# Attention inside two chained mixture-of-experts blocks: routing in front of the second head's scores, the product in front of the second turn, a batch's first output product later, and each pair's blocks read back at once

## The chip, the cores and the metric

The kernel runs on one core of one Trainium2 chip. The metric is the device time of one execution in microseconds, from three runs; each run is one execution of the whole program. TensorE is called PE in the profile, VectorE DVE, ScalarE ACT, GpSimd POOL, SyncE SP.

## The reference

Input x is 8 batches of 256 tokens of width 256. Two layers follow each other; each is x + FFN(COND(x)).

```python
x = x + L0_ffn(L0_cond(x, cond_64, ...), ...)      # MoE with 8 experts (A), MoE with 8 experts (B)
x = x + L1_ffn(L1_cond(x, fside, mask, ...), ...)  # attention (C), MoE with 16 experts (D)

def L1_cond(x, attn_bias, mask, g_in, null_attn_bias, null_kv, Wq, Wkv, Wo, g_out):
    xn = layernorm(x, g_in)                        # 16 query heads of width 64, one key/value head
    q = heads(xn @ Wq) * scale
    k, v = null row in front of (xn @ Wkv)         # 257 keys
    sim = q @ k.T + bias; sim = causal mask, key mask -> lowest
    out = softmax(sim) @ v
    return layernorm(heads together (out) @ Wo, g_out)
```

L1_ffn picks two of 16 experts for each token from the attention's output (its routing), so the routing of D for a batch can begin as soon as that batch's attention is done.

## The kernel before, in words

Everything is written by hand for each engine: an engine's program is one straight list, and semaphores order the engines among each other. Stages A and B come first; stage C (attention) takes the span from about 380 to 690 us; D follows.

Stage C treats one batch after the other (`batches`), and in a batch the heads in eight pairs, j = 0 to 7; p = 8b + j counts the 64 pairs. Each engine has a function for a batch (`pe_batch`, `act_batch`, `dve_batch`, `pool_batch`) whose loop over j is a software pipeline. In place p stand these steps:

- PE: scores of pair p+1 into psH or psHT (L1491), the sum (weights times values) of pair p-3 into psL (L1504, `pe_sum`, LAG = 3), queries of pair p+3 into psY (L1477), the output product of pair p-4 accumulated in psM (L1515, `pe_out`). The first output product of a batch has to wait until VectorE has read the previous batch's psM out (L1881, semaphore out_raw).
- DVE: transposes of the exponentials of pair p, head 1 (`dve_blocks`, L1863), scores plus bias with their minimum for pair p+1, head 1 (`dve_scores`, L1838), blocks of head 0 (L1863), reciprocals of the sums (L1845) and their transposes (L1852), the scaling of pair p-3's sum into c_oT (`dve_o`, L1872), scores of pair p+1, head 0, and last a piece of D's routing (`dve_dispatch`, L1917 to L1989). In some places the layer norm's statistics come between (`dve_row_*` L1799 to L1814, `dve_out_*` L1885 to L1900).
- ACT: exponentials of pair p+1, head 1 and head 0 (L1706), between them the copy of the queries (L1700), in some places normalization of rows (L1672), a copy for the routing (L1727), the mask (L1693) and the normalization of the outputs (L1680).
- POOL: mask minus bias of pair p+2, both heads (L2181), gating of the next batch's rows (L2195, L2199), rstd by a power (L2204, L2214), the weighting with g_out (L2225) and the indirect DMAs that dispatch tokens (L2247).
- SP: a transpose over 128 partitions is made of VectorE's transposes of 32x32 blocks and a trip through DRAM. `sp_store_blocks(p)` (L2341) writes the 512 KB of pair p from c_x1 to DRAM once the last transposes of the pair are done (128 rows, 4 KB each). `sp_load_blocks(p)` (L2350) reads them back in another order into c_x2 (512 pieces of 1 KB); it waits for the store to have landed and for the scaling of pair p-2, which frees the buffer. c_x1 and c_x2 have two buffers each; DVE's first transpose of pair p waits until store p-2 has landed.

SP's program for the stage is one list:

```python
for p in range(pairs):
    sp_store_blocks(sp, p)
    if p >= 1:
        sp_load_blocks(sp, p - 1)
```

Other DMAs run at the same time: expert weights of D on ACT's queue in batch 0 (one piece a pair), 4 MB of them on SP's queue in front of the first store, two loads of 256 KB a batch (L1723, ACT's queue), and four indirect DMAs a batch (POOL's queue).

Of the kernel before, what the change touches and what calls it, by code (L numbers as in the profile page):

```python
# [14 lines left out]
P = 128  # L15
# [212 lines left out]
def build(nc, io):  # L228
    ctx = ExitStack()
    with ctx:  # L230
# [6 lines left out]
        def carve(region, sizes):  # L237
# [81 lines left out]
            work, [512, 1024, 512, 4 * KEYS, 2 * KEYS, 4 * KEYS, DIM, 512, KEYS, 24, 1024, 2 * QT * DH, 4])  # L319
# [10 lines left out]
        c_oT = c_oT.rearrange("p (r n) -> p r n", r=2)  # L330
# [1177 lines left out]
        def pe_out(pe, p, j, b):  # L1508


            pe.wait_ge(C.o_ready, p + 1)
            if j == 0:
                wait(pe, C.out_raw, 2 * b)
            for i in range(QT):
                last = pe.matmul(psM[:, i * DIM:(i + 1) * DIM], c_oT[:, j % 2, i * P:(i + 1) * P], c_wo[:, j, :],  # L1515
                                 start=(j == 0 and i == 0), stop=(j == NPAIR - 1), skip_group_check=True)
            last.then_inc(C.wo_mm, 1)
# [90 lines left out]
        def pe_batch(pe, b, odd, first, last):  # L1608
            for j in range(NPAIR):
# [4 lines left out]
                if s >= 0:  # L1614
                    pe_sum(pe, s, s % NPAIR, s // NPAIR)
                if j == 1 and b >= 3:
                    pe_z_counts(pe, b - 3, psX)
# [15 lines left out]
                if s >= 1:  # L1633
                    pe_out(pe, s - 1, (s - 1) % NPAIR, (s - 1) // NPAIR)
# [107 lines left out]
        def act_batch(act, b, odd, first, last):  # L1742
            for j in range(NPAIR):
# [4 lines left out]
                if j == 3 and not last:  # L1748
                    act_normal_rows(act, b + 1)
                if j == 4 and not last:  # L1750
                    act_rowsT(act, b + 1, 1 - odd)
                if not (last and j + 3 >= NPAIR):
                    act_queries(act, p + 3, j + 3)
                if more:
                    act_exp(act, p + 1, j + 1, ORDER[1])
                act_load_d(act, p)
# [7 lines left out]
                if j == 2 and b >= 2:  # L1764
                    act_zT(act, b - 2)
# [100 lines left out]
        def dve_o(dve, p, j):  # L1866
# [4 lines left out]
            wait(dve, C.wo_mm, p - 1)  # L1871
            nc.vector.tensor_tensor(c_oT[:, j % 2, :].rearrange("p (i a q) -> p i a q", i=QT, a=4),  # L1872
# [186 lines left out]
        def dve_dispatch(dve, b, j, last):  # L2059
# [6 lines left out]
            if j == 2 and b >= 3:  # L2066
                dve_dest(dve, b - 3)
            if j == 3 and b >= 3:
                dve_counted(dve, b - 3)
            if j == 4 and b >= 2:  # L2070
                dve_best(dve, b - 2, 0)
            if j == 5 and b >= 2:
                dve_onehot(dve, b - 2, 0)
            if j == (5 if last else 6) and b >= 2:
                dve_best(dve, b - 2, 1)
            if j == (5 if last else 7) and b >= 2:
# [8 lines left out]
        def dve_batch(dve, b, odd, first, last):  # L2085
            for j in range(NPAIR):
# [7 lines left out]
                if j == 3 and not last:  # L2094
                    dve.wait_ge(C.row_step, 4 * b + 6)
                    dve_row_moments(dve, b + 1)
                    dve_row_variances(dve, b + 1)
                if more:
                    dve_scores_wait(dve, p + 1)
                    dve_scores(dve, p + 1, j + 1, ORDER[0])  # L2100
                dve_blocks(dve, p, j, ORDER[1])
                dve_sums(dve, p, j)
                dve_recs(dve, p)
                if s >= 0:
                    dve_o(dve, s, s % NPAIR)
                if j == 4 and not first:
                    dve_out_raw(dve, b - 1)

                if j == 2 and not last:
                    dve.wait_ge(B.combined, 2 * b + 4)  # L2110
                    dve_row_stats(dve, b + 1)
                if j == 5 and not first:
                    dve.wait_ge(C.out_step, 4 * b - 2)
                    dve_out_moments(dve, b - 1)
                    dve_out_variances(dve, b - 1)
                if more:
                    dve_scores(dve, p + 1, j + 1, ORDER[1])
                if j == 4 and not first:
                    dve.wait_ge(C.out_raw, 2 * b)
                    dve_out_stats(dve, b - 1)  # L2120
                if j == 3 and not last:
                    dve_row_shift(dve, b + 1)
                if j == 5 and not first:
                    dve_out_shift(dve, b - 1)
                dve_dispatch(dve, b, j, last)
# [124 lines left out]
        def pool_batch(pool, b, odd, first, last):  # L2250
            for j in range(NPAIR):
                p = 8 * b + j
                over = (j + 2) // NPAIR
                for n, o in enumerate(ORDER):
# [9 lines left out]
                    if h <= 2 * QT and not last:  # L2264
                        pool_pairs(pool, b + 1, h)
                    if j == 4 and n == 0:
# [12 lines left out]
                if j == 3 and not last:  # L2279
                    pool_row_rstd(pool, b + 1)  # L2280
# [72 lines left out]
        def sp_attention(sp):  # L2353
# [7 lines left out]
            for p in range(pairs):  # L2361
                sp_store_blocks(sp, p)
                if p >= 1:
                    sp_load_blocks(sp, p - 1)
            sp_load_blocks(sp, pairs - 1)
# [318 lines left out]
```

## Time and profile before

| what | us |
|---|---|
| three runs | 855.49, 839.8, 849.12 |
| their median | 849.12 |
| the profiled execution | 854.32 |
| its span, first to last instruction | 852.6 |
| mean granted clock of TensorE (share of full speed) | 0.92 |

The rows further down come from that one profiled execution. A row of a group or a timeline names line, engine, operation, and "written tile <- read tiles"; "x8" is a count, and brackets hold the idle time of the engine before it with what ended it. "PEclk" is the granted TensorE clock as a share of full speed. The queue q1 in the DMA view is SP's, q10 is ACT's, q0 is POOL's.

### The profile page before, as it was taken

What the parts mean: (1) busy time and instruction counts of PE and PEld (TensorE: products, weight loads), DVE (VectorE), ACT (ScalarE), POOL (GpSimd) and SP (SyncE); (2) the same over time, 40 slices, a digit from 0 to 9 for tenths busy, and PEclk for the clock granted to TensorE, in tenths of its full rate; (3) what the DMA queues carried; (4) which work ended last, traced back from release to release, by engine and by line L of the source; (5) the groups of instructions that cost most, each with busy time, mean ns of one, the idle gap of its engine ahead of it and who ended that gap; (6) DMA issues with size and microseconds to landing.
All of it is one profiled execution on the core that took longest, in us unless ns stands there. A gap on an engine that the chain in (4) does not pass through costs nothing. (4 is left out here: it accounts for less than half of the span.)

```text
span 852.6 us, 15701 instructions
## 1 busy us (share of the span) xinstructions
PE 737.8 (87%) x4481; PEld 568.2 (67%) x4482; DVE 476.1 (56%) x1751; ACT 361.0 (42%) x1068; POOL 422.6 (50%) x506
## 2 busy tenths in 40 slices
PE   8859995966999989985899989899989688988788
PEld 5349964655999989863566656566666445877665
DVE  2704464464232222246778899988989742444346
ACT  3526621233222222245546655565656315665302
POOL 1166315414453863245638486867857431344530
PEclk9889997966999999998999999999999778999979
DMA  9634533325979666188977777778868743444346
GB/s 315 257 99 143 136 111 112 100 87 166 351 255 356 215 180 205 56 296 309 336 260 246 240 237 249 253 249 265 264 205 273 237 148 96 119 122 139 107 142 197
DMA packets 101035, 173.41 MB, mean 203 GB/s; under 512 B 10976, under 2 KB 77792, under 8 KB 99936
## 3 DMA queue, kind: packets, MB, share of 16 engines
q1 hardware_dynamic: 79392, 117.03, 41.7%
q0 software_dynamic: 10944, 30.03, 11.5%
q10 hardware_dynamic: 10624, 25.46, 8.7%
q8 instruction: 34, 0.56, 0.3%
q14 instruction: 41, 0.34, 0.1%
HBM read 111.86 MB, written 60.62 MB: 202 GB/s over the span
## 5 line engine op out<-in xcount | busy, mean ns | idle before, releaser
L2181 POOL TENSOR_TENSOR work<-work,region_ac 128x386 f32<-128x386 f32 x128 | 119.4, 941 | 69.3 <-ACT work L1693 32.9
L1706 ACT ACTIVATE work<-work 128x129 f32<-128x129 f32 (+1 forms) x256 | 114.2, 448 | 89.2 <-DVE work L1838 87.3
L1863 DVE STREAM_TRANSPOSE region_bd<-work 128x384 f32<-128x384 f32 x128 | 73.3, 572 | 12.2 <-ACT work L1706 6.3
L1515 PE MATMUL psM<-region_ac,work 128*128 128x256 f32 x256 | 71.1, 403 | 9.7 <-DVE acc L1881 9.7
L1504 PE MATMUL psL<-region_bd,work 128*64 128x256 f32 (+1 forms) x512 | 61.6, 365 | 19.0 <-DMA region_bd<-c_blocks 17.0
L1367 POOL DMA_INDIRECT d_pairs<-work,home x47 | 45.9, 976 | 64.0 <-DVE home_f L1119 44.9
L1477 PE MATMUL psY<-work,region_ac 128*128 128x256 f32 x256 | 71.3, 401 | 2.2 <-ACT work L1700 2.2
L1504 PEld LDWEIGHTS psL<-region_bd,work 128*64 128x64 f32 x512 | 34.1, 147 | 55.1 <-DMA region_bd<-c_blocks 27.2
L1356 POOL DMA_INDIRECT b_pairs<-work,home x39 | 38.1, 977 | 56.9 <-DVE work L1063 54.6
L860 PE MATMUL psH<-work,region_bd 128*128 128x128 f32 x472 | 62.8, 290 | 3.9 <-ACT work L968 2.2
L1348 POOL DMA_INDIRECT work<-in_x,inv x39 | 37.1, 953 | 55.5 <-DVE inv L1276 35.0
L1037 ACT ACTIVATE work<-work 128x512 f32<-128x512 f32 x39 | 24.6, 630 | 93.6 <-DVE work L1056 70.4
L860 PEld LDWEIGHTS psH<-work,region_bd 128*128 128x128 f32 x472 | 59.8, 205 | 5.7 <-ACT work L968 3.4
L1515 PEld LDWEIGHTS psM<-region_ac,work 128*128 128x128 f32 x256 | 50.0, 200 | 19.7 <-DVE work L1872 10.9
L1429 POOL DMA_INDIRECT work<-a_slots,slot_u x32 | 31.3, 978 | 48.1 <-DMA a_slots<-work 26.7
L1348 POOL DMA_INDIRECT work<-y_scratch,inv x39 | 37.8, 968 | 35.0 <-DVE inv L1276 21.4
L1477 PEld LDWEIGHTS psY<-work,region_ac 128*128 128x128 f32 x256 | 44.0, 192 | 12.2 <-issue 4.8
L1838 DVE CUSTOM_DVE_ANT_0 work<-psHT,work 128x129 f32<-128x129 f32 (+1 forms) x128 | 40.2, 350 | 17.9 <-PE psHT L1491 16.6
L1706 ACT ACTIVATION_READ_ACCUMULATOR work<-work 128x1 f32 x256 | 47.9, 187 | 0.0
L1838 DVE CUSTOM_DVE_ANT_0 work<-psH,work 128x129 f32<-128x129 f32 (+1 forms) x128 | 40.1, 350 | 4.9 <-PE psH L1491 4.7
L913 PE MATMUL psHT<-work,region_bd 128*128 128x128 f32 x304 | 37.6, 276 | 4.6 <-ACT work L1026 3.4
L913 PE MATMUL psH<-work,region_bd 128*128 128x128 f32 x320 | 41.3, 285 | 0.0
(367 smaller groups left out, 1608.3 us busy)
## 6 DMA issues: line engine op xcount, KB each, us to landing
c_blocks<-region_bd SPq DMA_DIRECT2D x64, 512.0 KB
region_bd<-c_blocks SPq DMA_DIRECT2D x64, 512.0 KB
region_bd<-in_b_w ACTq DMA_DIRECT2D x37, 512.0 KB
work<-d_rows SPq DMA_DIRECT2D x47, 132.0 KB
a_slots<-work SPq DMA_DIRECT2D x19, 256.0 KB
region_bd<-in_b_w SPq DMA_DIRECT2D x1, 4096.0 KB, 15.4
region_bd<-in_d_w SPq DMA_DIRECT2D x1, 4096.0 KB, 19.7
work<-d_pairs SPq DMA_DIRECT2D x16, 256.0 KB
```

The source lines that it names most:

```text
L860: last = pe.matmul(pair_h[p % DEEP][:, t % PAIR, j, :], f.w_in(j, k, t), xT[:, p % DEEP, t % PAIR, k, :], start=(k == 0), stop=(k == KD - 1))
L913: last = pe.matmul(ffn_h[u % RING][:, j * P:(j + 1) * P], f.w_in(j, k, u % RING), b_xT[:, u % 2, k, :], start=(k == 0), stop=(k == KD - 1))
L1348: pool.indirect_dma_start(out=slot_rows(f, t), out_offset=None, in_=st.src, in_offset=bass.IndirectOffsetOnAxis(ap=inv[:, t:t + 1], axis=0 ...
L1356: pool.indirect_dma_start(out=st.pair_dram, out_offset=bass.IndirectOffsetOnAxis(ap=home[:, t:t + 1], axis=0), in_=ys[:, t % RING, :], in_ ...
L1367: pool.indirect_dma_start(out=st.pair_dram, out_offset=bass.IndirectOffsetOnAxis(ap=home[:, t:t + 1], axis=0), in_=d_ys[:, t % ROWS, :], i ...
L1477: last = pe.matmul(psY[:, 0:SEQ], c_wq[:, c, j * P:(j + 1) * P], c_xnT[:, odd, c, :], start=(c == 0), stop=(c == KD - 1))
L1504: last = pe.matmul(psL[DH * o:DH * o + DH, queries].rearrange("p (i a q) -> p i a q", a=4, q=32), c_v[:, b % 2, n, :], weights[:, o, block ...
L1515: last = pe.matmul(psM[:, i * DIM:(i + 1) * DIM], c_oT[:, j % 2, i * P:(i + 1) * P], c_wo[:, j, :], start=(j == 0 and i == 0), stop=(j == ...
L1706: nc.scalar.activation(c_p[:, j % 2, o, a:z], c_sc[:, o, a:z], ACT.Exp, scale=-1.0, bias=c_min[:, o, i:i + 1], accum_out=c_sum[:, j % 2, o ...
L1838: last = nc.vector.tensor_tensor_reduce(c_sc[:, o, a:z], psS[j % 2][:, o, a:z], c_bm[:, 2 * (j % 2) + o, a:z], 1.0, -LOWEST, ALU.add, ALU. ...
L1863: nc.vector.transpose(out=c_x1[:, p % 2, :, (QT + 1) * o:(QT + 1) * (o + 1), :].rearrange("p b i q -> p i b q"), in_=c_p[:, j % 2, o, 1:1 ...
L2181: pool.tensor_tensor(c_bm[:, 2 * (j % 2) + o, :], c_mp, c_bias[:, 2 * j + o, :], ALU.subtract).then_inc(C.bm_ready, 1)
```

## The change

- SP reads a pair's blocks back directly behind their store: store(p), load(p), store(p+1), and so on.
- DVE scales the sum of pair p-3 in front of the blocks of head 0 instead of behind the reciprocals. c_oT has three buffers instead of two, and `dve_o` waits for the output product of three pairs ago.
- DVE's routing step stands in front of the scores of head 0. Its pieces are spread anew: destinations in place 1 instead of 2, first choice in 5 and 6 instead of 4 and 5, second choice in 7 instead of 6 and 7.
- The statistics of the next batch's rows are taken in place 2 behind the scores, moments and variances with them (before: place 3); POOL's rstd stands between its two steps in place 3.
- ACT normalizes the next batch's rows behind the exponentials of head 0 in place 3, and copies for the routing in front of them in place 2.
- PE leaves out the output product in place 4 (a batch's first) and makes it in place 5, in front of the next one.

The core of the diff:

```diff
-            work, [512, 1024, 512, 4 * KEYS, 2 * KEYS, 4 * KEYS, DIM, 512, KEYS, 24, 1024, 2 * QT * DH, 4])
+            work, [512, 1024, 512, 4 * KEYS, 2 * KEYS, 4 * KEYS, DIM, 3 * SEQ, KEYS, 24, 1024, 2 * QT * DH, 4])
...
-                last = pe.matmul(psM[:, i * DIM:(i + 1) * DIM], c_oT[:, j % 2, i * P:(i + 1) * P], c_wo[:, j, :],
+                last = pe.matmul(psM[:, i * DIM:(i + 1) * DIM], c_oT[:, p % 3, i * P:(i + 1) * P], c_wo[:, j, :],
...
+                if j == 5:
+                    pe_out(pe, 8 * b, 0, b)
...
-                if s >= 1:
+                if s >= 1 and j != 4:
                     pe_out(pe, s - 1, (s - 1) % NPAIR, (s - 1) // NPAIR)
...
-                if j == 3 and not last:
-                    act_normal_rows(act, b + 1)
...
+                if j == 2 and b >= 2:
+                    act_zT(act, b - 2)
                 if more:
                     act_exp(act, p + 1, j + 1, ORDER[1])
+                if j == 3 and not last:
+                    act_normal_rows(act, b + 1)
...
-                if j == 2 and b >= 2:
-                    act_zT(act, b - 2)
...
-            wait(dve, C.wo_mm, p - 1)
+            wait(dve, C.wo_mm, p - 2)
...
-            if j == 2 and b >= 3:
                 dve_dest(dve, b - 3)
...
-            if j == 4 and b >= 2:
+            if j == 5 and b >= 2:
                 dve_best(dve, b - 2, 0)
-            if j == 5 and b >= 2:
+            if j == (5 if last else 6) and b >= 2:
                 dve_onehot(dve, b - 2, 0)
-            if j == (5 if last else 6) and b >= 2:
+            if j == (5 if last else 7) and b >= 2:
                 dve_best(dve, b - 2, 1)
-            if j == (5 if last else 7) and b >= 2:
                 dve_onehot(dve, b - 2, 1)
...
-                if j == 3 and not last:
-                    dve.wait_ge(C.row_step, 4 * b + 6)
-                    dve_row_moments(dve, b + 1)
-                    dve_row_variances(dve, b + 1)
                 if more:
                     dve_scores_wait(dve, p + 1)
                     dve_scores(dve, p + 1, j + 1, ORDER[0])
+                if s >= 0:
+                    dve_o(dve, s, s % NPAIR)
                 dve_blocks(dve, p, j, ORDER[1])
                 dve_sums(dve, p, j)
                 dve_recs(dve, p)
-                if s >= 0:
-                    dve_o(dve, s, s % NPAIR)
                 if j == 4 and not first:
                     dve_out_raw(dve, b - 1)
-
-                if j == 2 and not last:
-                    dve.wait_ge(B.combined, 2 * b + 4)
-                    dve_row_stats(dve, b + 1)
                 if j == 5 and not first:
                     dve.wait_ge(C.out_step, 4 * b - 2)
                     dve_out_moments(dve, b - 1)
                     dve_out_variances(dve, b - 1)
+                dve_dispatch(dve, b, j, last)
+                if j == 3 and not last:
+                    dve_row_shift(dve, b + 1)
                 if more:
                     dve_scores(dve, p + 1, j + 1, ORDER[1])
+                if j == 2 and not last:
+                    dve.wait_ge(B.combined, 2 * b + 4)
+                    dve_row_stats(dve, b + 1)
+                    dve.wait_ge(C.row_step, 4 * b + 6)
+                    dve_row_moments(dve, b + 1)
+                    dve_row_variances(dve, b + 1)
...
-                if j == 3 and not last:
-                    dve_row_shift(dve, b + 1)
...
-                dve_dispatch(dve, b, j, last)
...
+                    if j == 3 and n == 0 and not last:
+                        pool_row_rstd(pool, b + 1)
...
-                if j == 3 and not last:
-                    pool_row_rstd(pool, b + 1)
...
             for p in range(pairs):
                 sp_store_blocks(sp, p)
-                if p >= 1:
-                    sp_load_blocks(sp, p - 1)
-            sp_load_blocks(sp, pairs - 1)
+                sp_load_blocks(sp, p)
```

## Rows read from the trace of the kernel before

**Rows 1.** The page, section 1: busy time of each engine over the span.
```profile
PE 737.8 (87%) x4481; PEld 568.2 (67%) x4482; DVE 476.1 (56%) x1751; ACT 361.0 (42%) x1068; POOL 422.6 (50%) x506
```

**Rows 2.** Table of stretches, batches 0 and 4: length, busy us (instructions) by engine, clock, DMA.
```profile
381.35:419.21 37.86, 27.07 (x169) 18.34 (x170) 25.52 (x117) 20.24 (x79) 22.81 (x30) 0.91 0.94 331
...
531.67:569.94 38.27, 34.30 (x225) 23.69 (x224) 34.18 (x150) 21.96 (x83) 28.39 (x37) 0.96 0.76 248
```

**Rows 3.** The stores' line by itself: duration ns, first and last start us.
```profile
L2341 SPq DMA_DIRECT2D c_blocks<-region_bd x64: 319/319/333, 381.3 to 674.8; - x64
```

**Rows 4.** Timeline of TensorE, 595 to 603: start us, duration us, then the group.
```profile
595.42 0.93 PE L1491 MATMUL psHT<-region_bd,work 64*128 64x129 f32 x8
...
599.00 0.93 PE L1491 MATMUL psH<-region_bd,work 64*128 64x129 f32 x8
```

**Rows 5.** Waits (us in total, times, longest) and one routing group, 380 to 690.
```profile
DVE work L1838 <- PE psHT L1491: 16.6, 15, 2.5
DVE region_bd L1863 <- ACT work L1706: 5.2, 6, 1.1
PE psL L1504 <- DMA region_bd<-c_blocks: 17.0, 12, 7.9
PE psM L1515 <- DVE acc L1881: 9.7, 7, 2.0
...
L1933 DVE TENSOR_TENSOR region_bd<-region_bd 128x32 f32<-128x32 f32 x12 | 6.4, 532 | 0.4
```

**Rows 6.** Timeline, 574 to 580, and the table of stretches behind it (clock: third figure from the right).
```profile
574.21 0.39 SPq L2350 DMA_DIRECT2D region_bd<-c_blocks  x1
...
579.96 0.87 PE L1504 MATMUL psL<-region_bd,work 128*64 128x256 f32 x8 [1.35 <-DMA region_bd<-c_blocks]
...
582.00:584.00 2.00, 2.00 (x7) 1.62 (x6) 1.97 (x12) 0.99 (x4) 2.00 (x4) 0.58 0.03 13
```

**Rows 7.** Timeline of SyncE's queue, 598 to 602, and its waits in the stage.
```profile
598.15 0.32 SPq L2341 DMA_DIRECT2D c_blocks<-region_bd  x1
598.57 0.40 SPq L2350 DMA_DIRECT2D region_bd<-c_blocks  x1
601.74 0.32 SPq L2341 DMA_DIRECT2D c_blocks<-region_bd  x1
...
SPq L2350 <- DMA c_blocks<-region_bd: 8.0, 4, 5.9
```

**Rows 8.** DMA view of 598.9 to 600.5, then of 600.5 to 602.4: packets by size.
```profile
DMA packets 135, 0.52 MB, mean 328 GB/s; under 512 B 2, under 2 KB 10, under 8 KB 134
...
DMA packets 539, 0.54 MB, mean 285 GB/s; under 512 B 30, under 2 KB 534, under 8 KB 538
```

**Rows 9.** Timeline, 381 to 394: the first two stores, the first load, the first sum.
```profile
381.35 3.10 SPq L2341 DMA_DIRECT2D c_blocks<-region_bd  x2
390.34 0.37 SPq L2350 DMA_DIRECT2D region_bd<-c_blocks  x1
...
394.11 1.12 PE L1504 MATMUL psL<-region_bd,work 128*64 128x256 f32 x4 [7.89 <-DMA region_bd<-c_blocks]
```

**Rows 10.** Timeline, 419 to 428: a load, the store behind it, and what each releases.
```profile
419.63 0.39 SPq L2350 DMA_DIRECT2D region_bd<-c_blocks  x1
...
422.80 0.32 SPq L2341 DMA_DIRECT2D c_blocks<-region_bd  x1
...
426.32 0.87 PE L1504 MATMUL psL<-region_bd,work 128*64 128x256 f32 x8 [1.75 <-DMA region_bd<-c_blocks]
...
428.07 0.37 SPq L2350 DMA_DIRECT2D region_bd<-c_blocks  x1
```

**Rows 11.** DMA queues, 380 to 690: packets, MB, share of 16 engines.
```profile
q10 hardware_dynamic: 4992, 6.05, 5.6%
q0 software_dynamic: 1152, 3.25, 2.9%
```

**Rows 12.** Timeline, 674 to 688: the last store and the last sum.
```profile
674.82 0.32 SPq L2341 DMA_DIRECT2D c_blocks<-region_bd  x1
...
687.60 1.12 PE L1504 MATMUL psL<-region_bd,work 128*64 128x256 f32 x8
```

More of the change, by code:

```diff
@@ L329, in build @@
         c_p = c_p.rearrange("p (r o n) -> p r o n", r=2, o=2)
-        c_oT = c_oT.rearrange("p (r n) -> p r n", r=2)
+        c_oT = c_oT.rearrange("p (r n) -> p r n", r=3)
         c_min = c_small[:, 0:4].rearrange("p (o i) -> p o i", o=2)
@@ L1870, in dve_o @@
             wait_dma(dve, C.blocks_loaded, 0, p)
-            wait(dve, C.wo_mm, p - 1)
-            nc.vector.tensor_tensor(c_oT[:, j % 2, :].rearrange("p (i a q) -> p i a q", i=QT, a=4),
+            wait(dve, C.wo_mm, p - 2)
+            nc.vector.tensor_tensor(c_oT[:, p % 3, :].rearrange("p (i a q) -> p i a q", i=QT, a=4),
                                     psL[:, 0:SEQ].rearrange("p (i a q) -> p i a q", i=QT, a=4),
```

## The prediction

> **What bounds the kernel now.** I read the busy shares first. TensorE is busy for 87% of the span and no other engine for more than 56% [rows 1], but that mixes stages. The change touches only the attention stage, so the next view is the table of stretches there: in the fifth batch (531.67 to 569.94) TensorE is busy for 34.30 of 38.27 us and VectorE for 34.18 [rows 2]. Two engines are nearly full and neither is quite full, so they take turns waiting. SyncE's issue rows give the pace: 64 stores from 381.3 to 674.8, that is 293.5 us in 63 steps, 4.66 us a pair [rows 3]. The timeline of TensorE shows what it could do: where nothing holds it, one pair's scores start at 595.42 and the next at 599.00, 3.58 us a pair [rows 4]. So about 1.1 us of each pair is lost somewhere.
>
> The waits say where. VectorE waits 16.6 us for the scores in psHT and 5.2 for exponentials; TensorE waits 17.0 us for the loaded blocks and 9.7 for VectorE to read psM out [rows 5]. One such wait can be followed: the load issued at 574.21 releases the product at 579.96 after 1.35 us of idleness, and shortly after, between 582 and 584, the granted clock is 0.58 instead of 1.00 (the lower level, 1.2 GHz, for most of it) [rows 6]. TensorE's pause thus costs twice. The transfers are late since SyncE issues the load of pair p only behind the store of pair p+1: store 598.15, load (of the pair before) 598.57, next store 601.74 [rows 7].
>
> **The change, part by part.**
>
> *Blocks read at once.* SyncE now runs store(p), load(p), store(p+1). Nothing is added in instructions or bytes: 64 stores and 64 loads of 512 KB stay. What is added is a wait: load(p) waits for store(p) to land and for the product of pair p-2 to have been scaled, and SyncE is in order, so store(p+1) is queued behind that wait. VectorE's transposes of pair p+3 wait for store(p+1), TensorE's sum for its load. In the old order this wait was nearly always over when it was reached, because a whole pair lay between.
>
> How long is one turn of this loop? It has three pieces.
> (a) A load that has the queue to itself. SyncE issues one at 390.34, and TensorE, idle for 7.89 us, is released by it at 394.11 [rows 9]: 3.77 us.
> (b) The store behind it. It is ready long before (VectorE's work is 34.2 us for 8 pairs [rows 2]), so it is issued at once, 0.42 us after the load (the distance of 598.15 and 598.57 is that of two issues in a row [rows 7]). Do its packets pass the load's? The windows of the DMA view say no, for the opposite order: the load is issued at 598.57, yet from 598.9 to 600.5 the packets are all but ten of the store's size (4 KB), and from 600.5 to 602.4, 534 of 539 are small ones, the load's [rows 8]. The queue is worked off in order. What a store costs behind a load is seen at 419 to 428: the load of 419.63 releases TensorE at 426.32, the store of 422.80 releases SyncE at 428.07 [rows 10], 1.75 us later.
> (c) SyncE's own issue times lie inside (a).
> A turn is so 3.77 + 1.75 = 5.5 us. By the other bound, if the store's packets didn't wait at all, a turn would be 0.42 us and a store alone: its packets end 2.35 us after its issue [rows 7, 8], so 2.8 us and a landing time the views do not show. I take 5.5: the rows in (b) are the same two transfers on the same queue.
> The order of packets is shown here for a load behind a store only. The Trainium skill, page "DMA: Bandwidth & Descriptors", section "Queues, rings and completion order", states it for every pair: on each engine the descriptors are consumed in ring order. By that rule a store waits for a load just as well; without it the turn could be as short as the lower bound above.
>
> 5.5 is above the 4.66 of today, and each pair needs one turn, so the loop sets the pace whatever the engines do. Sum: from the first store of batch 1 (419.21) to the last (674.82) there are 55 steps in 255.6 us; 55 x 5.5 = 302.5, +47. In batch 0 the first store, issued at 381.35, has landed at 390.34 (the 4 MB of expert weights go first), and now the second store, today issued by 384.45, waits for that [rows 9]. From 390.75 there are 7 turns to the first store of batch 1: 429.3 instead of 419.2, +10. Other queues take engine time too: 5.6% and 2.9% of the stage's 310 us [rows 11], 0.41 us a pair. Today it fits into gaps; in a closed loop up to two thirds of it count (the share of a turn in which the blocks' packets run), 0 to 17 us. I take 8. At the end, today 12.8 us lie between the last store and the last sum (674.82, 687.60) [rows 12]; then it is about 5.1 (store behind a load) + 3.8 (load alone), -4. Together +61 us.
>
> *Product in front of the second turn* (VectorE's scaling of the sum, L1872, moves in front of the blocks of head 0, with a third buffer for its result). The same 61 instructions. It lets load(p) go earlier by the length of a block's transposes and sums, and fills the time in which the exponentials of head 0 run, the cause of the 5.2 us [rows 5]. The price is a wait for the sum in front of the blocks, at most one sum of 0.87 us [rows 6]. Alone: from -5 (those waits gone) to +26 (half of the pairs wait a whole sum). In the loop of 5.5 us VectorE has the slack, so I count 0.
>
> *Routing in front of the second head's scores.* The same instructions in another place, destinations one pair earlier, second choices later. The scores of head 0 start later by the routing, and its exponentials with them. A single product of the first choice averages 532 ns [rows 5] over 12, so one pair's share is 0.5 to 1.5 us. 0 as long as VectorE waits for blocks anyway; if that cover were gone, up to 1 us in half of the pairs, +30, against what the removed waits give.
>
> *A batch's first outputs held back* (the first output product goes to place 5, two in one pair). It removes the 9.7 us in which TensorE waits for psM [rows 5] and adds nothing; TensorE has 1.9 us of slack in a 5.5 us pair. 0 here. The statistics of the next batch's rows behind the scores, their rstd earlier on GpSimd, the normalization and the turn's copy moved around ScalarE's exponentials: likewise 0 here; alone they would remove short waits of VectorE.
>
> The profiled execution took 854.32 us, the three runs have a median of 849.12. The sum is made against the profile: 854.3 + 61 = 915. Against the median: 849.1 + 61 = 910; since the natural 3.77 may have held some of the weights' traffic, I lower this slightly, to **906 us**.
>
> **Rivals.**
>
> *Faster: the removed waits count, the loop does not bind.* The place is SyncE's load issue. If a store behind a load landed within 4.2 us of its issue, a turn would be under 4.66. Then TensorE's 17.0 + 9.7 us, VectorE's 16.6 + 5.2 [rows 5] and the half-clock stretches would be open for gain. VectorE has 34.2 us of work in 38.3 [rows 2]; half of the difference over seven batches and what the first loses less gives -14 to -30: 827 us. For it: loads are the latest thing in the slowest places [rows 6]. Against it: the order of packets [rows 8] and the 1.75 us behind a load [rows 10]. The point from which it decides is a turn of 4.66 us.
>
> *No difference: the loop binds a little.* A turn of 4.4 to 4.9 us, if half of the store's transfer ran beside the load's (1.6 of 3.5 us of packets hidden). The pace stays at today's, the gains in the slow places pay for batch 0: 850 us.
>
> *Worse than forecast: the clock.* TensorE's pauses grow to 1.4 us or more in every pair, the length after which the clock fell at 582 [rows 6]. At the lower clock its pair needs about 7.2 us (twice 3.58), over 5.5. If a third of the pairs ran so, +35: 940. Against: batch 0 has a clock share of 0.91 although TensorE is idle for 10.8 us of it [rows 2].
>
> **How the numbers follow.** The loop as forecast 0.66 (its own range 885 to 930), with the clock on top 0.11, no difference 0.09, faster 0.14. The range leaves out the faster case and most of the clock's: 845 to 930. Two per cent is about what a measurement of this kernel can tell from no change: slower 0.77, same 0.09, faster 0.14.
>
> **What would show it.** Right: SyncE's load waits for its own store in nearly every pair (today 8.0 us in total, 4 times [rows 7]), store to store is 5.3 to 5.8 us in the steady batches, each store is issued 0.4 us after a load, VectorE's blocks wait for stores, and TensorE's wait for psM is gone. Wrong: stores less than 4.7 us apart; or a store that lands within 4 us though a load is just ahead of it; or a pace of 5.5 with waits that end at the sum or the scores instead of at the store.

## The result, and the profile after

The kernel with the change takes 923.43 us (median of 4 runs, 919.83 to 926.55), the kernel before 846.79 us beside it on the same chip (4 runs, 839.80 to 855.49). The ratio is 1.093, with a 95% interval of 1.084 to 1.102: 9.3% slower, 76.6 us by the medians. The profiled execution took 923.82 us, its span is 922.1 us, so profile against profile the loss is 922.1 - 852.6 = 69.5 us. Some executions of one kernel take longer as a whole than the rest (here 855.49 us of the kernel before), and the ratios and their intervals, in the whole document, are made without those, so a ratio can differ from the quotient of the two medians beside it.

The page's first section for the kernel after, which answers to [rows 1]:

```profile
PE 754.1 (82%) x4481; PEld 578.7 (63%) x4482; DVE 472.1 (51%) x1751; ACT 361.0 (39%) x1068; POOL 422.5 (46%) x506
```

No instruction was added. VectorE does the same work in a longer span. TensorE's busy time rose by 16 us with the same 4481 instructions: it ran more of them at the lower clock (mean granted clock 0.911, before 0.920). The stores' line by itself, against [rows 3]:

```profile
L2339 SPq DMA_DIRECT2D c_blocks<-region_bd x64: 319/457/815, 376.8 to 751.0; - x64
```

From the first store to the last it is now 374.2 us instead of 293.5, that is 5.94 us a pair instead of 4.66. These 80.7 us are more than the whole loss; what offsets the rest is listed further down, under "The sum". The waits of the stage say what each engine waits for (us in total, times, longest), against [rows 5] and the last of [rows 7]:

```profile
DVE region_bd L1865 <- DMA c_blocks<-region_bd: 115.9, 57, 6.3
PE psL L1504 <- DMA region_bd<-c_blocks: 84.4, 49, 9.0
DVE work L1840 <- PE psHT L1491: 0.3, 1, 0.3
...
SPq L2348 <- DMA c_blocks<-region_bd: 260.0, 60, 9.1
```

Before, VectorE's transposes (L1863, now L1865) did not wait for stores except once; now they do in 57 of 64 pairs. SyncE's load waits for its own store in 60 pairs, 260.0 us in all, where it was 8.0 us in 4. TensorE's wait for psM is gone, and VectorE's for the scores nearly so: both engines now arrive early at nearly everything except a transfer (VectorE's scaling still waits 8.8 us in 3 pairs for the sum). One turn and the start of the next, from the timeline at the start of the fifth batch (start us, duration us, what it is, in brackets the idle time before it and its releaser):

```profile
568.68 0.37 SPq L2348 DMA_DIRECT2D region_bd<-c_blocks  x1
568.76 0.58 DVE L1865 STREAM_TRANSPOSE region_bd<-work 128x384 f32<-128x384 f32 x1 [1.46 <-DMA c_blocks<-region_bd]
569.15 0.46 SPq L2339 DMA_DIRECT2D c_blocks<-region_bd  x1
...
573.16 1.20 PE L1504 MATMUL psL<-region_bd,work 128*64 128x256 f32 x8 [2.01 <-DMA region_bd<-c_blocks]
574.38 0.37 SPq L2348 DMA_DIRECT2D region_bd<-c_blocks  x1
574.46 0.58 DVE L1865 STREAM_TRANSPOSE region_bd<-work 128x384 f32<-128x384 f32 x1 [1.81 <-DMA c_blocks<-region_bd]
574.84 0.46 SPq L2339 DMA_DIRECT2D c_blocks<-region_bd  x1
```

Read it as a circle. The load goes out at 568.68 and the store of the next pair 0.47 us behind it. That store lands before 574.38; its landing releases both the next load (574.38) and VectorE's next transposes (574.46), since these write the buffer that the store reads. The load's landing releases the sum at 573.16. A turn is 574.38 - 568.68 = 5.70 us, and no step of the circle is computing. The DMA view of 569.7 to 571.9 and then of 571.9 to 574.2 shows the order of packets, in answer to [rows 8]:

```profile
DMA packets 329, 0.34 MB, mean 154 GB/s; under 512 B 1, under 2 KB 328, under 8 KB 329
...
DMA packets 343, 0.71 MB, mean 309 GB/s; under 512 B 31, under 2 KB 216, under 8 KB 343
```

The store was issued at 569.15, yet until 571.9 all but one of 329 packets are small ones, the load's. The store's large ones come as the load's run out: by the packet records the first starts at 571.77, the rest from 571.92 on, and the load's last ends at 572.76. So a store does wait for a load ahead of it, as a load does for a store in [rows 8]; that a ring's descriptors are consumed in order is also what the Trainium skill, page "DMA: Bandwidth & Descriptors", section "Queues, rings and completion order", states, and here the trace agrees.

### The profile page after: what moved, and what is told of

Read it like the earlier page. It is cut to its first block and busy times, and to the rows that moved or that the text cites. A ratio compares the mean times of both kernels' runs of the same rounds, so it can differ in the third digit from the quotient of the medians.

```text
span 922.1 us, 15701 instructions
## 1 busy us (share of the span) xinstructions
PE 754.1 (82%) x4481; PEld 578.7 (63%) x4482; DVE 472.1 (51%) x1751; ACT 361.0 (39%) x1068; POOL 422.5 (46%) x506
## 5 line engine op out<-in xcount | busy, mean ns | idle before, releaser
L1865 DVE STREAM_TRANSPOSE region_bd<-work 128x384 f32<-128x384 f32 x128 | 73.3, 573 | 117.1 <-DMA c_blocks<-region_bd 115.9
L1477 PE MATMUL psY<-work,region_ac 128*128 128x256 f32 x256 | 83.1, 454 | 2.1 <-ACT work L1702 2.1
L1515 PE MATMUL psM<-region_ac,work 128*128 128x256 f32 x256 | 79.9, 444 | 0.0
L1515 PEld LDWEIGHTS psM<-region_ac,work 128*128 128x128 f32 x256 | 56.7, 227 | 11.7 <-issue 2.4
L860 PEld LDWEIGHTS psH<-work,region_bd 128*128 128x128 f32 x472 | 59.6, 205 | 3.9 <-ACT work L968 2.3
L1477 PEld LDWEIGHTS psY<-work,region_ac 128*128 128x128 f32 x256 | 50.6, 219 | 14.3 <-issue 5.2
L913 PEld LDWEIGHTS psH<-work,region_bd 128*128 128x128 f32 x320 | 40.0, 203 | 1.9 <-issue 1.9
```

The lines of the kernel that those rows point to most:

```text
L860: last = pe.matmul(pair_h[p % DEEP][:, t % PAIR, j, :], f.w_in(j, k, t), xT[:, p % DEEP, t % PAIR, k, :], start=(k == 0), stop=(k == KD - 1))
L913: last = pe.matmul(ffn_h[u % RING][:, j * P:(j + 1) * P], f.w_in(j, k, u % RING), b_xT[:, u % 2, k, :], start=(k == 0), stop=(k == KD - 1))
L1477: last = pe.matmul(psY[:, 0:SEQ], c_wq[:, c, j * P:(j + 1) * P], c_xnT[:, odd, c, :], start=(c == 0), stop=(c == KD - 1))
L1515: last = pe.matmul(psM[:, i * DIM:(i + 1) * DIM], c_oT[:, p % 3, i * P:(i + 1) * P], c_wo[:, j, :], start=(j == 0 and i == 0), stop=(j == ...
L1865: nc.vector.transpose(out=c_x1[:, p % 2, :, (QT + 1) * o:(QT + 1) * (o + 1), :].rearrange("p b i q -> p i b q"), in_=c_p[:, j % 2, o, 1:1 ...
```

## The experiments

Each kernel was compared with the kernel before on one chip, but not all of them on the same one, and the kernel before is not equally long everywhere (842.80, 846.79 and 851.16 us, and 791.17 us beside experiments 5 to 8). So times are compared with the kernel before beside them, and stage lengths by the distance between stores.

**1. The order of reads alone.** The kernel before with this edit and nothing else:

```diff
             for p in range(pairs):
                 sp_store_blocks(sp, p)
-                if p >= 1:
-                    sp_load_blocks(sp, p - 1)
-            sp_load_blocks(sp, pairs - 1)
+                sp_load_blocks(sp, p)
```

> The kernel before with SyncE's new order alone (store p, load p); nothing else of the change. Theory (closed loop: the load waits for its own store, the next store is queued behind the load): stores 5.7 to 6.0 us apart, VectorE waiting for stores by about 100 us in the stage, time 915 to 930 us, the whole loss of the change. Rival (the loss comes from the moved engine steps, or from both together): below 890 us.

Measured: 927.90 us, before 851.16; ratio 1.101 (1.082 to 1.120). The stores' line by itself:

```profile
L2341 SPq DMA_DIRECT2D c_blocks<-region_bd x64: 319/457/1938, 377.0 to 751.9; - x64
```

and the waits of the stage:

```profile
DVE region_bd L1863 <- DMA c_blocks<-region_bd: 115.6, 57, 6.3
...
SPq L2350 <- DMA c_blocks<-region_bd: 195.2, 59, 9.1
SPq L62 <- DVE work L1872: 104.6, 61, 2.2
```

Same pace (374.9 / 63 = 5.95 us), same waits. This one line of SyncE's program is the whole loss. SyncE waits less for its store and more for VectorE's scaling than in the full change (195.2 and 104.6 us against 260.0 and 40.9), since the scaling comes later in a pair here. It waits for the scaling first and for the store behind that, and the two together are the same (299.8 and 300.9 us), so the store ends the wait in both kernels and an earlier scaling buys nothing inside the loop.

**2. Everything else, with the old reads.** The change in full with the edit above undone.

> The changed kernel with SyncE's old order (store p, then load p-1). Theory: the loss is gone and the moved steps give what they can without the loop: 820 to 840 us, ratio 0.97 to 0.99; TensorE's wait for psM (9.7 us before) gone, VectorE's wait for exponentials (5.2 us) gone. Rival (the moved steps cost by themselves, by GpSimd's operations that stall routing operations in front of the scores): over 850 us.

Measured: 850.26 us; ratio 1.007 (1.001 to 1.013). A miss: I expected 820 to 840. The pace is that of before (384.6 to 677.8, 4.65 us a pair), though the wait for psM is gone. Its waits:

```profile
PE psL L1504 <- DMA region_bd<-c_blocks: 29.0, 21, 8.6
DVE work L1840 <- PE psHT L1491: 11.9, 9, 2.9
DVE work L1874 <- PE psL L1504: 10.7, 27, 1.7
```

The waits have new names instead of being fewer: the scaling, now in front of the blocks, waits for the sum 27 times between the first and the last store (before: twice, 1.5 us), and TensorE waits 29.0 us for loaded blocks where it was 17.0. Experiments 5 to 8 and 11 and 12 take this apart.

**3. Another queue for the stores.** ScalarE issues the stores, and SyncE only loads; the rest is the change in full.

```diff
                 act_load_d(act, p)
+                sp_store_blocks(act, p)
...
             for p in range(pairs):
-                sp_store_blocks(sp, p)
                 sp_load_blocks(sp, p)
```

> The changed kernel with the 64 stores issued by ScalarE, behind the exponentials of head 0 of each place; SyncE issues the loads alone, each as soon as its store has landed. Same bytes. Theory (the turn is long since store p+1 waits in line for load p, in SyncE's program and in the queue): the turn opens, stores follow VectorE's pace, 4.2 to 4.7 us apart, 815 to 845 us; loads are issued about 3 us behind their store. Rival (engines' transfer time or DRAM turnaround between the store's end and the load is the limit, whoever issues): pace stays over 5.3 us, time over 890 us.

Measured: 862.49 us; ratio 1.022 (1.006 to 1.039). Store to store it is (686.4 - 380.7) / 63 = 4.85 us. The rival is refuted, but the 815 to 845 us were missed too: most of the loss is gone and no gain came. Its waits:

```profile
DVE region_bd L1866 <- DMA c_blocks<-region_bd: 23.7, 20, 6.5
...
SPq L2349 <- DMA c_blocks<-region_bd: 142.6, 59, 18.6
```

Taking the store out from behind the load opens the loop: VectorE's wait for stores falls from 115.9 to 23.7 us. But it does not vanish, and TensorE waits 44.5 us for loaded blocks in 27 pairs. The packets of both queues use the same 16 engines, and a store issued while a load runs still has its first packets up to 2.3 us after its issue in the fourth batch, against 0.83 where nothing is in its way. The edit takes the store out of two lines at once, SyncE's program and its queue, and what each was worth is not separated. In the change in full a store is issued a median 3.6 us after VectorE's last transposes for it (0.03 us before) and its first packet starts 2.7 us after its issue (0.82 before).

**4. Half of each load.** The change in full, but a load reads two of the four groups of blocks: 256 pieces of 1 KB.

```diff
-            sp.dma_start(c_x2[:, p % 2, :, :, :]..., blocks_dram[r]...
+            sp.dma_start(c_x2[:, p % 2, 0:2, :, :]..., blocks_dram[r, 0:2]...
```

> The changed kernel, each load reads only half of its blocks (the first two of four groups, 256 pieces of 1 KB instead of 512); half of the weights used by the sums are then old ones. Theory (a store behind a load waits until the load's packets are through): the turn falls by the packets left out, 256 x 46 ns / 16 = 0.74 us, to about 5.0 to 5.2 us a pair, time about 875 to 885 us. Rival (the turn is fixed latencies, packets side by side): turn unchanged within 0.2 us, time over 910 us.

Half of the weights in its sums are left over from earlier pairs. Measured, one execution: 859.42 us, before 851.16; stores 383.0 to 689.8, 4.87 us apart. More was gained than expected (875 to 885 us): the median turn from the second batch on is 4.3 us, 1.4 less than with the whole load, where 0.74 was expected. I took this for a sign that the number of pieces sets the length of a load, and tested that next.

**5. The outputs held back alone** (with the third buffer; the kernel before otherwise).

```diff
                     pe_sum(pe, s, s % NPAIR, s // NPAIR)
+                if j == 5:
+                    pe_out(pe, 8 * b, 0, b)
...
-                if s >= 1:
+                if s >= 1 and j != 4:
                     pe_out(pe, s - 1, (s - 1) % NPAIR, (s - 1) // NPAIR)
```

> The kernel before with one part of the change: the first output product of a batch in place 5, and the third buffer that it needs. If the 9.7 us in which TensorE waits for psM are on the path: that wait is gone and the time falls by 5 to 10 us, to 840 to 845. If VectorE's work sets the pace in those places, the wait only moves to another row (the scores or the loaded blocks) and the time stays within 3 us of before. The rival in which two output products in one pair delay the next scores: 852 to 856, with a longer wait of VectorE for psHT in place 5.

Measured: 784.93 us, before 791.17 on this chip; ratio 0.994 (0.990 to 0.998). The wait for psM is gone, and some 5 us with it. The times expected were those of a chip on which the kernel before takes about 850 us; the gain of 5 to 10 us and the missing wait are what came.

**6. Old reads, and the routing back in its old places.** Experiment 2 with VectorE's routing at the end of a pair again and its steps in their old pairs; the other moves stay.

```diff
-                dve_dispatch(dve, b, j, last)
                 if j == 3 and not last:
                     dve_row_shift(dve, b + 1)
...
                     dve_out_shift(dve, b - 1)
+                dve_dispatch(dve, b, j, last)
```

> The change without the new order of reads and with the routing (VectorE's choices and destinations) back at the end of a pair and in its old places; product in front, outputs held back, statistics moved stay. If it is the routing in front of the second head's scores that gives back what the removed waits bring: 835 to 845, and the 2.8 us between the reciprocals and the second head's scores in place 7 are gone. If the wait for the sum in front of the blocks of head 0 (15.6 us, 29 times, with the old reads) gives it back: 848 to 856, with that wait as it was.

Measured: 784.58 us; ratio 0.991 (0.988 to 0.994), as the first branch had it (835 to 845 us of about 850). The edit undoes two things at once, the routing's position in a pair and the pairs in which its steps stand.

**7. Half of each piece.** The change in full; a load reads 512 pieces of 512 B.

```diff
-            sp.dma_start(c_x2[:, p % 2, :, :, :]..., blocks_dram[r]...
+            sp.dma_start(c_x2[:, p % 2, :, 0:4, :]..., blocks_dram[r, :, :, 0:128]...
```

> The change in full, but each load reads only the first half of every 1 KB piece: as many pieces (512), half of the bytes. The probabilities and factors of the other half are left over from other work, so the product computes on wrong data. If the length of a load goes by its pieces, nothing changes against the change in full: 915 to 925, stores 5.8 to 5.95 us apart. If it goes by its bytes, as much is gained as when half of the pieces were left out: 855 to 865, stores 4.8 to 4.9 apart.

Its sums run on old data in the other half. Measured, one execution: 804.52 us, before 791.17 beside it, stores 4.85 us apart: the branch of the bytes, by the distance of the stores. SyncE's queue in its fifth batch:

```profile
507.21 0.37 SPq L2348 DMA_DIRECT2D region_bd<-c_blocks  x1
507.68 0.46 SPq L2339 DMA_DIRECT2D c_blocks<-region_bd  x1
511.47 0.37 SPq L2348 DMA_DIRECT2D region_bd<-c_blocks  x1
```

and the same queue in experiment 4:

```profile
502.17 0.37 SPq L2348 DMA_DIRECT2D region_bd<-c_blocks  x1
502.63 0.42 SPq L2339 DMA_DIRECT2D c_blocks<-region_bd  x1
506.52 0.37 SPq L2348 DMA_DIRECT2D region_bd<-c_blocks  x1
```

A turn is 4.26 us here and 4.35 there: it makes no difference whether the pieces or their number are halved. My idea of experiment 4 falls: at 512 B to 1 KB these loads take time by bytes. In the packet records of either halved form their packets run from 1.0 to 2.65 us after the issue (medians), for 256 KB, and in the full change from 1.0 to 4.1 us, for 512 KB: 160 to 170 GB/s. That is no fixed rate of such a load: in the kernel before, where the load stands behind a store, the same 512 packets take a median 2.35 us, and in [rows 8] nearly all of a load's fall within 1.9 us (285 GB/s). The stores' packets, of 4 KB, take a median 2.1 us in the full change for the same 512 KB, 1.8 at the fastest. Both halved kernels have a turn under the 4.66 us of before, and both are, by their single executions, still a little slower than before (1.7% and 1.0%); their stores are 4.85 and 4.87 us apart on average. The loop only binds less often.

**8. Stores on ScalarE in the kernel before.** The edits of experiment 3, made in the kernel before (all loads on SyncE, each at its own pair).

> The kernel before, only that ScalarE issues the stores (behind head 0's exponentials and its own loads of a pair); SyncE issues loads alone, each as soon as its store has landed and the buffer is free. If TensorE's 17.0 us of waiting for loaded blocks come from loads that SyncE issues late: 838 to 846, with that wait under 8 us. If ScalarE's instructions issue the stores too late, or loads and stores of two queues share the engines and lengthen each other: 850 to 862, with VectorE waiting for stores (0 before) as in the kernel with the change.

Measured: 805.24 us, before 791.17; ratio 1.019 (1.014 to 1.024). Its waits:

```profile
PE psL L1504 <- DMA region_bd<-c_blocks: 29.4, 21, 8.1
DVE region_bd L1864 <- DMA c_blocks<-region_bd: 28.9, 19, 6.0
```

Nothing is gained by loads on a queue of their own: TensorE's wait for loaded blocks is 29.4 us, not less than the 17.0 of [rows 5], and VectorE waits for stores in 19 pairs. Both causes that were expected are in the trace: ScalarE issues a store a median 1.35 us after VectorE's last transposes for it (0.03 us before), and its first packet then starts a median 1.56 us after the issue (0.82 before). How much each costs isn't separated, and so this run does not show whether reading earlier loses by itself when no store stands behind the load.

**9. The change in full, on another chip.**

> The change in full, so that the kernels with half of each load's bytes or pieces, and the old reads, can be set beside it on one chip. If the closed loop of SyncE is what the time goes by, the stores are again 5.8 to 6.0 us apart and the time is 1.08 to 1.10 of before, whichever chip it is (65 to 77 us more). If the loss hung on the chip of the first runs (its lower clock, its slower memory), the ratio is nearer to one: 1.03 to 1.06.

Measured: 922.78 us, before 842.80; ratio 1.097 (1.092 to 1.102). Stores 379.2 to 748.4, 5.86 us apart. The loss belongs to the kernel and not to one chip.

**10. Product in front alone** (with the third buffer).

```diff
+                if s >= 0:
+                    dve_o(dve, s, s % NPAIR)
                 dve_blocks(dve, p, j, ORDER[1])
                 dve_sums(dve, p, j)
                 dve_recs(dve, p)
-                if s >= 0:
-                    dve_o(dve, s, s % NPAIR)
```

> The kernel before with one part of the change: VectorE scales the sum in front of the blocks of head 0, with a third buffer for the result. My forecast had -5 to +26 for it alone. If the wait for exponentials in front of head 0's blocks (5.2 us) and the later release of the load count: 0.990 to 0.997 of before, that wait gone and TensorE's wait for loaded blocks shorter. If the wait for the sum in front of the blocks counts: 1.003 to 1.02, with a new wait of VectorE's scaling for TensorE's sum of 10 us or more.

Measured: 843.21 us; ratio 1.001 (0.999 to 1.004). Its waits in the stage:

```profile
DVE work L1872 <- PE psL L1504: 18.2, 23, 4.4
PE psM L1515 <- DVE acc L1881: 10.0, 7, 1.6
DVE work L1838 <- PE psHT L1491: 6.2, 6, 2.0
...
DVE region_bd L1863 <- ACT work L1706: 2.7, 6, 0.5
```

The wait for exponentials is halved (5.2 to 2.7) and that for scores falls from 16.6 to 6.2, but the scaling waits for the sum in 23 pairs; between the first and the last store this is 12.1 us in 21 pairs, before 1.5 us in 2. The signs of both branches came and the time is between them: the gain and the price cancel.

**11 and 12. The routing's place, side by side.** The kernels of experiments 2 and 6 again, on one chip.

> Everything but the new order of reads, beside the same kernel with the routing back in its old places. On another chip it took 1.007 of before, and that one 0.991. If the routing's place is the difference: 1.003 to 1.010 here, and 1.0 to 1.8 per cent above its neighbour. If the two ratios differed only because of the chips: both within half a per cent of each other.

> Old reads, routing back in its old places; product in front, outputs held back and statistics moved stay. If this is the best form of the change, it takes 0.987 to 0.995 of before again, 1.0 to 1.8 per cent under its neighbour with the routing in front of the scores. If it was the chip: as its neighbour, within half a per cent.

Measured: 844.53 us with the routing in front of the second head's scores (ratio 1.003, 1.000 to 1.006), 835.67 us with it back (ratio 0.992, 0.989 to 0.995). The routing's new place costs 8.9 us, 1.1%, on the same chip. The waits, first with the routing in front:

```profile
ACT work L1702 <- PE psY L1477: 31.1, 22, 2.8
PE psL L1504 <- DMA region_bd<-c_blocks: 29.8, 17, 8.6
DVE work L1840 <- PE psHT L1491: 13.0, 10, 2.3
...
DVE work L1840 <- PE psH L1491: 4.5, 7, 1.7
```

and with it back at the end of a pair:

```profile
PE psL L1504 <- DMA region_bd<-c_blocks: 25.3, 22, 8.7
ACT work L1702 <- PE psY L1477: 24.9, 19, 3.1
...
DVE work L1840 <- PE psHT L1491: 7.7, 8, 2.8
```

From the starts of VectorE's first transposes in each place of the later five batches, the places 6 and 7 together take 11.17 us with the routing in front and 8.55 with it back, places 1 and 3 together 8.86 and 6.91, while places 2 and 4 take 8.88 and 11.86; over all eight it is 37.5 against 35.9 us. In places 6 and 7 steps of the choices now stand ahead of scores. Whether it is that position or the new spread over the pairs that costs is argued from the stretch below and not shown, for the two runs differ in both. One such stretch, in experiment 2:

```profile
565.04 0.14 DVE L1933 TENSOR_REDUCE region_bd<-region_bd 128x2 f32<-128x32 f32 x1
565.22 0.45 DVE L1935 TENSOR_TENSOR region_bd<-region_bd 128x32 f32<-128x32 f32 x1
565.57 1.41 POOL L2223 TENSOR_TENSOR region_bd<-acc,g_out 128x256 f32<-128x256 f32 x2
565.70 0.65 DVE L1937 TENSOR_TENSOR region_bd<-region_bd,rank 128x32 f32<-128x32 f32 x1
...
566.95 1.02 POOL L2179 TENSOR_TENSOR work<-work,region_ac 128x386 f32<-128x386 f32 x1
567.07 0.94 DVE L1950 TENSOR_TENSOR oh<-region_bd 128x32 f16<-128x32 f32 x1
567.93 0.28 DVE L1840 CUSTOM_DVE_ANT_0 work<-psH,work 128x129 f32<-128x129 f32 x1
...
568.60 0.41 ACT L1708 ACTIVATE work<-work 128x129 f32<-128x129 f32 x1 [2.78 <-DVE work L1840]
```

The second head's scores start at 567.93, 2.9 us after the routing began, and ScalarE's exponentials have been idle for 2.78 us when they are released. The tiny products last long only beside a GpSimd operation: 0.94 us at 567.07, ending with GpSimd's own. In this trace the 128x32 products that overlap no GpSimd instruction take 0.19 us, all 7 of them, and the 49 that overlap one take 0.19 to 0.94. The group means show the same, with the operation that suffers depending on the place: L1937 takes 385 ns on average with the routing in front and 194 with it back, L1935 298 and 524. That VectorE and GpSimd exclude each other on a shared pair of ports when VectorE has two inputs in SBUF and GpSimd reads SBUF is what the Trainium skill, page "SBUF — State Buffer", section "SBUF: two separate sides", states; the rows agree. Here moving such an operation moved the collision and did not remove it.

## Why the prediction was right, point by point

**The bound.** Right. I forecast that SyncE's own order would close a loop of one load and one store and set the pace whatever the engines do. The signs named in advance came: SyncE's load waits for its store in 60 pairs, each store goes out 0.47 us after a load, VectorE's blocks wait for stores, the psM wait is gone. Experiment 1 shows that this part alone is the loss. The steady distance was forecast as 5.3 to 5.8 us; the median over the pairs from the second batch on is 5.71.

**The length of a turn.** The term mis-sized, though its error is small: 5.5 us forecast, 5.86 measured on average (322.1 us from 428.93, the first store of the second batch, to 751.03, in 55 steps). Both pieces were off, in opposite directions, and that the errors nearly cancel is luck. Piece (a), the load alone, was read from one row as 3.77 us [rows 9]. In the profile after, the sum starts 4.48 us after its load in the turn shown above, and the median over all 64 pairs is 4.52, the fastest 3.90. I had taken the one load that was the fastest of the 64 of the kernel before. Piece (b), the store behind it, is 574.38 - 573.16 = 1.22 us and not 1.75. Together 5.70 in a turn with nothing in its way. The rest is in part other traffic. Of the 55 turns, 22 hold packets of ScalarE's or GpSimd's queue; together they are 8.3 us longer than as many median turns without, and most of the turns over 6.2 us (5 of 7) stand beside ScalarE's pair loads, such as that from 639.99 to 647.42. But this one in the fifth batch, nearly the longest, does not:

```profile
610.30 0.46 SPq L2339 DMA_DIRECT2D c_blocks<-region_bd  x1
617.24 0.37 SPq L2348 DMA_DIRECT2D region_bd<-c_blocks  x1
617.70 0.46 SPq L2339 DMA_DIRECT2D c_blocks<-region_bd  x1
```

With the load at 609.84 this is a turn of 7.40 us, and all but one of its 673 packets are SyncE's; why it is long stays open. Over 55 turns the mean lies 0.16 us above 5.70, that is 9 us, beside the 8 I had put down; the missing 11 us are the turn's own 0.2.

**The sum.** Forecast and measured, profile to profile: 55 turns with their side traffic +55, measured 322.1 - 255.6 = +66.5. Batch 0 +10, measured +14.3 (from 376.75 to 428.93 it takes 52.18 us, before 37.86 [rows 2]); its first turn took 9.9 us and the next seven 5.7 to 6.6. The end -4, measured from these rows:

```profile
751.03 0.46 SPq L2339 DMA_DIRECT2D c_blocks<-region_bd  x1
...
760.04 1.55 PE L1504 MATMUL psL<-region_bd,work 128*64 128x256 f32 x8 [1.54 <-DMA region_bd<-c_blocks]
```

9.0 us instead of 12.8 [rows 12], -3.8. The attention began 4.6 us earlier than in the profile of before and what follows it took 2.9 less; no part of the change touches either, and the runs of before alone lie 15.7 us apart. The total is 66.5 + 14.3 - 3.8 - 4.6 - 2.9 = 69.5, forecast 61. So the forecast is nearer to the total than to the part it was made for: the attention stage alone lost 66.5 + 14.3 - 3.8 = 77.0 us, about the 76.6 between the medians, and is 16 over the forecast, 11.5 of it in the 55 turns and 4.3 in batch 0. Lowering 910 to 906 at the end, because the load of [rows 9] might have been slowed by the weights, went the wrong way: it was the fastest one.

**Product in front, routing, outputs, statistics, costed at 0.** Right in the loop: the full change (1.093 and 1.097) and its first part alone (1.101) have the same ratio within their intervals. Outside of it the parts are not all nothing. The product alone is nothing (experiment 10, inside the -5 to +26 that I gave). The outputs held back give about 5 us (experiment 5; 2 to 8 by its interval), half of the 9.7 us of waiting. The routing costs 8.9 us (experiments 11 and 12); I had named up to 30 for it if its cover were gone. That the old reads would show a gain of 10 to 30 us, which I expected before experiment 2, was wrong: a wait in a list is not a gain to be had in full, for here VectorE and TensorE mostly exchanged waits when one was removed.

**The rivals.** The faster one and the one without a difference fall with the turn: 5.7 us is far from 4.66. With a shorter turn the faster one would probably still not come true: with turns of 4.3 us (experiments 4 and 7, one execution each, and half of the bytes left out besides) the kernel is 1.0 and 1.7% slower than before, which is nearly the rival without a difference. The clock's rival is present and hidden. The granted clock falls from 0.91 in the first batch and 0.96 in the fifth [rows 2] to 0.84 and 0.86, in the table of stretches (the clock is third from the right):

```profile
376.75:428.93 52.18, 34.62 (x193) 23.00 (x194) 26.15 (x122) 21.80 (x84) 26.08 (x34) 0.84 0.75 250
...
569.15:617.70 48.55, 37.35 (x222) 25.55 (x220) 33.84 (x150) 22.24 (x82) 29.11 (x38) 0.86 0.58 196
```

TensorE is busy for 37.35 us of 48.55 here and was for 34.30 of 38.27 [rows 2]. Its query products (L1477) average 454 ns over the kernel instead of 401. Still it has 11 us of slack in the batch, and no step of the circle is TensorE's, so I take the lower clock for a consequence of the waits and not for a part of the loss; no run holds the clock fixed to show it.

**A version better than both.** The change without the new reads and without the new place of the routing takes 0.991 and 0.992 of before on two chips (intervals 0.988 to 0.994, and 0.989 to 0.995). That is 7 us, most of it, by experiment 5, from the outputs held back.

## What to carry to other kernels

Before transfers are put closer together on one in-order queue, follow what each issue waits for: where a load waits for a store and the next store stands behind that load, the two form a circle, and its length (a whole load and a whole store, with both landings) is the pace as soon as it is longer than the engines' work on one pair. A pair of work between a store and its load costs latency that is hardly waited for here (17.0 us in 12 of 64 pairs); taking it away costs throughput. And take the length of a transfer from all of its kind, not from the one that is easiest to see.

## What the runs showed that was not expected

- A load of 512 KB in pieces of 1 KB that starts on an empty queue runs at about 170 GB/s in its packets, and with 512 B pieces and half of the bytes, or with half of the pieces, at the same rate. Behind a store, in the kernel before, the same load is quicker in its packets (a median 2.35 us instead of 3.0). What holds the loads at the lower rate isn't settled by these runs: the piece size between 512 B and 1 KB isn't it, and the DMA engines aren't full (they are busy for 60.8% of 569.7 to 571.9, with nearly nothing but the load).
- Stores on a second queue are not free of the loads of the first: in the fourth batch of experiment 3 their first packets come 0.83 us after the issue when the engines are free, and up to 2.3 us where a load is running.
- VectorE's 128x32 products take 0.19 us where no GpSimd instruction runs beside them and up to 0.94 us where one does (experiment 2), so a kernel's order of instructions on one engine changes the durations on it.
- The same kernel before takes 791 us on one chip and 843 to 851 us in the other comparisons. The ratio of the change in full and that of its best form came out the same on two chips each (1.093 and 1.097, 0.991 and 0.992).
